# Gated delta rule on one core: five entries of a hand-written slot table moved

## The reference, cut to what matters

```
def step(S, inp):                       # one token; S is 96 x 192 for each of 8 heads
    q_t, k_t, v_t, g_t, b_t = inp
    S = S * jnp.exp(g_t)[..., None, None]
    v_old = jnp.einsum('bhk,bhkv->bhv', k_t, S)
    delta = (v_t - v_old) * b_t[..., None]
    S = S + jnp.einsum('bhk,bhv->bhkv', k_t, delta)
    o_t = jnp.einsum('bhk,bhkv->bhv', q_t, S)
    return (S, o_t)
...
g_out = (h @ Wg).reshape(B, T, H, dv)
o = _rmsnorm(o, onorm_w) * jax.nn.silu(g_out)
x = x + o.reshape(B, T, H * dv) @ Wo
```

## Time and profile before

| | us |
|---|---|
| median of 3 runs | 3595.34 (3591.72 to 3601.11) |
| profiled execution, its own time | 3593.64 |
| its span in the trace | 3591.9 |
| delta stage's stretch with both units and chunks in flight | about 180 to 1400 of the span |

### The profile page before, as it was taken

How to read it: one execution, slowest core, us unless ns; L and a number is a source line. 1 busy time by engine, 2 the same in 40 slices (tenths; PEclk the granted TensorE clock), 3 DMA queues, 4 the chain that set the end, 5 groups by cost and what they waited for, 6 DMA issues and landing times. The chain is left out here.

```text
span 3591.9 us, 86970 instructions
## 1 busy us (share of the span) xinstructions
PE 3217.1 (90%) x32714; PEld 2426.5 (68%) x32714; DVE 2675.9 (74%) x5718; ACT 2061.6 (57%) x4823; POOL 1796.2 (50%) x1631
## 2 busy tenths in 40 slices
PE   4899999999999999798999999987988799899998
PEld 3678888788788888655666566655665466656665
DVE  5677777777777777477777677776999577767775
ACT  3566666666666666325765477623443466536662
POOL 3355555555555555235664366622222566436662
PEclk9699999999999999999999999997999899999999
DMA  4111111111111110142222212231221122222132
GB/s 130 25 27 27 27 26 27 27 29 27 28 28 37 30 26 13 32 121 54 49 70 68 67 46 52 69 97 46 72 63 41 47 53 69 64 72 48 47 75 74
DMA packets 406989, 182.42 MB, mean 51 GB/s; under 512 B 233552, under 2 KB 381744, under 8 KB 404016
## 3 DMA queue, kind: packets, MB, share of 16 engines
q1 hardware_dynamic: 406576, 176.87, 20.1%
HBM read 94.20 MB, written 40.12 MB: 37 GB/s over the span
## 5 line engine op out<-in xcount | busy, mean ns | idle before, releaser
L1205 POOL TENSOR_TENSOR delta_cv<-delta_cv,delta_last_tap 96x256 f32<-96x256 f32 (+1 forms) x384 | 331.8, 864 | 557.0 <-DVE delta_cv L1646 557.0
L1985 POOL TENSOR_TENSOR g_a_rn<-g_a_clip,held_minus_half 128x16 f32<-128x16 f32 x64 | 186.3, 2911 | 240.7 <-DVE g_a_clip L2250 240.7
L1985 POOL TENSOR_TENSOR f_a_rn<-f_a_clip,held_minus_half 128x16 f32<-128x16 f32 x64 | 186.3, 2910 | 237.9 <-DVE f_a_clip L2250 209.7
L2202 ACT ACTIVATE g_a_pr<-g_ps,g_a_nb,g_a_rn 128x128 f32<-128x128 f32 x512 | 185.5, 468 | 125.4 <-DVE g_a_nb L2284 125.4
L2202 ACT ACTIVATE f_a_pr<-f_ps,f_a_nb,f_a_rn 128x128 f32<-128x128 f32 x512 | 185.5, 468 | 124.8 <-DVE f_a_nb L2284 124.8
L1474 ACT ACTIVATE delta_cv<-delta_ps,delta_conv_qk 96x256 f32<-96x256 f32 x256 | 121.4, 474 | 229.6 <-PE delta_ps L1299 228.5
L1638 DVE SCALAR_TENSOR_TENSOR delta_cv<-delta_ps,delta_conv_qk,delta_cv 96x256 f32<-96x256 f32 x256 | 122.1, 477 | 170.8 <-ACT delta_last_tap L1476 168.8
L1243 PE MATMUL delta_ps<-delta_state,delta_qk 96*128 96x192 f32 x1024 | 197.4, 336 | 27.1 <-issue 26.5
L1243 PEld LDWEIGHTS delta_ps<-delta_state,delta_qk 96*128 96x128 f32 x1024 | 164.5, 191 | 37.2 <-issue 33.8
L1988 POOL TENSOR_TENSOR f_a_rot_c<-f_a_rot_c,f_a_rot_s 128x1024 f32<-128x1024 f32 x64 | 150.5, 2351 | 0.0
L1988 POOL TENSOR_TENSOR g_a_rot_c<-g_a_rot_c,g_a_rot_s 128x1024 f32<-128x1024 f32 x64 | 150.4, 2350 | 0.0
(11 more groups left out here) (349 smaller groups left out, 10288.5 us busy)
## 6 DMA issues: line engine op xcount, KB each, us to landing
f_a_vm<-f_a_v SPq DMA_DIRECT2D x128, 130.0 KB, 2.3
g_a_vm<-g_a_v SPq DMA_DIRECT2D x128, 130.0 KB, 2.3
delta_gd<-delta_dram_row SPq DMA_DIRECT2D x16, 1024.0 KB, 4.9
window_vm<-window_v SPq DMA_DIRECT2D x64, 128.0 KB, 2.3
f_m_x<-y SPq DMA_DIRECT2D x24, 256.0 KB, 3.5
delta_dram_inv<-delta_sub SPq DMA_DIRECT2D x16, 256.0 KB, 2.1
f_m_more<-x SPq DMA_DIRECT2D x16, 256.0 KB, 4.1
held_table<-const_rotation SPq DMA_DIRECT2D x4, 1024.0 KB, 6.7
```

The lines of the kernel that those rows point to most:

```text
L1205: pool.tensor_tensor(cv[0:M, t % 3], cv[0:M, t % 3], last_tap[0:M, t % 3], ALU.add).then_inc(summed.sem, 1)
L1985: pool.tensor_tensor(rn[:, u % 2], clip[:, u % 2], minus_half[:], ALU.pow).then_inc(rn_sb.sem, 1)
L2202: e = act.activation(pr[:, u % 2, half, i, :], ps[:, score_bank(u, half), i * P:(i + 1) * P], ACT.Exp, bias=nb[:, u % 2, half, i:i + 1], s ...
```

## The change

Five edits to the table of the delta stage; no instruction is added or removed.

1. The query scores of the second half of the heads (`kq`, i = 1) move from slots 18 and 19 to 21 and 22: on PE eight matmul passes each, on DVE one L1679 each. With them SP's load of the next unit's decays moves from slot 20 to 23.
2. The norms `inv`, `brk`, `nbrk`, `npb` (DVE) move from slot 19 to 20, and `bvr` from 19 to 17.
3. POOL's merge factors `bm` move from slot 22 to 21.
4. For even chunks POOL's power (L1229) moves from slot 21 to 22, and its two norm products (L1236) from 21, 22 to 23, 24.
5. ACT takes the first gate of the odd chunk (slot 22) ahead of `light` instead of behind it.

```
-    KK_AT, KQ_AT = ((6, 7), (9, 10)), ((13, 14), (18, 19))
+    KK_AT, KQ_AT = ((6, 7), (9, 10)), ((13, 14), (21, 22))
+    POWER_AT, NORMED_AT = (16, 15), (17, 15)
...
-                n = unit(t, K_NORM + 8)
+                n = unit(t, K_NORM + 7)
                 if n is not None:
                     rates_sb.need(pool, n)
...
-                C = chunk(t, 15)
-                if C is not None:
-                    ostat_sb.need(pool, C)
-                    o_normed.need(pool, C - 1)
-                    pool.tensor_tensor(of[:], ostat[:, 1, :], minus_half[:, 0:H], ALU.pow).then_inc(of_sb.sem, 1)
...
+                for cc in range(2):
+                    C = chunk_of(t, POWER_AT[cc], cc)
                     if C is not None:
...
+                        pool.tensor_tensor(of[:], ostat[:, 1, :], minus_half[:, 0:H], ALU.pow).then_inc(of_sb.sem, 1)
+                    for i in range(2):
+                        C = chunk_of(t, NORMED_AT[cc] + i, cc)
...
-            def misc(t):
+            def gates(t, ahead):
                 for cc in range(2):
                     for k, when in enumerate(GATE_AT[cc]):
                         C = chunk_of(t, when, cc)
-                        if C is not None:
+                        if C is not None and ahead == (k == 0 and cc == 1):
...
                 products_of(t)
+                gates(t, True)
                 if t > 0:
                     light(t - 1)
+                gates(t, False)
                 misc(t)
...
-                n = unit(t, K_NORM + 5)
+                n = unit(t, K_NORM + 6)
...
+                n = unit(t, K_NORM + 3)
+                if n is not None:
+                    p = n % 2
                     rn_sb.need(dve, n)
                     dve.tensor_tensor(bvr[:, p], rn[:, p], ex[:, BETA, 2 * n:2 * n + 2, :].rearrange("p t h -> p (t h)"),
```

More of the change, by code:

```diff
@@ L1224, in _ @@
                         pool.tensor_tensor(mine, mine, gate[:, HB * i * DV:HB * (i + 1) * DV], ALU.mult).then_inc(o_gated.sem, 1)
-                C = chunk(t, 15)
-                if C is not None:
-                    ostat_sb.need(pool, C)
-                    o_normed.need(pool, C - 1)
-                    pool.tensor_tensor(of[:], ostat[:, 1, :], minus_half[:, 0:H], ALU.pow).then_inc(of_sb.sem, 1)
-                for i in range(2):
-                    C = chunk(t, 15 + i)
-                    if C is not None:
[L1233 to L1237, removed]
+                for cc in range(2):
+                    C = chunk_of(t, POWER_AT[cc], cc)
+                    if C is not None:
+                        ostat_sb.need(pool, C)
+                        o_normed.need(pool, C - 1)
+                        pool.tensor_tensor(of[:], ostat[:, 1, :], minus_half[:, 0:H], ALU.pow).then_inc(of_sb.sem, 1)
+                    for i in range(2):
+                        C = chunk_of(t, NORMED_AT[cc] + i, cc)
+                        if C is not None:
+                            of_sb.need(pool, C)
+                            o_gated.need(pool, C)
+                            mine = o[:, cc, HB * i:HB * i + HB, :]
+                            pool.tensor_tensor(mine, mine, of[:, HB * i:HB * i + HB].unsqueeze(2).to_broadcast([P, HB, DV]), ALU.mult)\
+                                .then_inc(o_normed.sem, 1)
         @block.tensor
@@ L1503, in misc @@
                             emptied(act.activation(gate[:, k * 512:(k + 1) * 512], ps[:, bank, :], ACT.Silu), ("gate", C, k))
+            def misc(t):
                 for cc in range(2):
```

## The result

| | before | after |
|---|---|---|
| median, us (lowest to highest) | 3597.54 (3591.72 to 3601.11), 4 runs | 3686.45 (3676.84 to 3692.95), 4 runs |
| profiled execution: span | 3591.9 | 3690.1 |
| PE busy / idle in the span | 3217.1 / 374.8 | 3276.5 / 413.6 |
| ratio, 95% interval | | 1.0247 (1.0216 to 1.0278) |

A forecast was written before the change was run, and what follows sets the result against it. The prediction took PE, busy 90% of the span, as the bound, with only its idle time to win or lose. Waits +15.0, clock +12.0 and late loads -2.4 gave +24.6 on 3593.6 us: 3618, range 3582 to 3642.

The forecast's parts named there:

- First half of the walk: Around slots 19 and 20, PE idles 0.6 and then 1.75 us instead of 1.33; the second kd wait goes.
- the walk: Unit 7 stepped through in the new order from the old rows: +1.0 us per unit, +15.0 over 15 units.
- The gate waits for DVE: At slot 22's gate, PE waits 2.05 us for DVE to read the scores of slot 21.
- the norms, which now stand in between, add 718.88 - 718.16 = 0.72: On DVE between the taps of slots 20 and 21, the moved norms add 0.72 us.
- The waiting term: PE's waits in units 1 to 15: 15 x 1.0 = +15.0 us, range +9 to +21.
- The clock term: PE's half-clock stretches around the new gaps: 0.8 us per unit, +12.0 in all; bounds 0 and 3.4 per unit.
- Out of that go the two POOL-made waits: After the gate, PE's waits in slots 23 and 24, 1.03 and 1.05 us by start times, disappear.
- Late loads: In units 5 and 14, x4's wait for its DMA and the clock falls behind it go: -2.4 us.
- Rival 1: The walk holds but PE is not throttled by such short gaps: 3607 us, chance 0.20.
- Rivals 2 and 3: Rival 2: no gate wait, 3575 us, chance 0.20; rival 3: waits only change places, 3592 us, chance 0.10.
- rival 2: At slot 22's gate, the scores' bank comes back in time and the kernel is faster: 3575 us, chance 0.20.
- The direction: Whole kernel: slower was given chance 0.57, same 0.23, faster 0.20.

The follow-up runs named there:

- e1: The kernel after with the norms inv, brk, nbrk and npb back in slot 19; 3606.21 us, ratio 1.0026.
- e6: The kernel after with POOL's gate product of 768 columns written as four products of one head each; 3631.24 us, ratio 1.0104.
- e2: The kernel before with the norms edit alone: inv, brk, nbrk, npb in slot 20, bvr in slot 17; 3642.37 us, ratio 1.0118.
- e4: The kernel before with edits 3, 4 and 5 alone, scores and norms in their old slots; 3576.75 us, ratio 0.9940.
- e3: The kernel before with the second scores alone moved to slots 21 and 22; 3610.74 us, ratio 1.0024.
- e5: The kernel after with the second scores back in slots 18 and 19; 3641.12 us, ratio 1.0122.
- e7: e4 with only the odd chunk's second scores moved, from slot 19 to 22; 3608.20 us, ratio 1.0026.
- e12: e4 with only the even chunk's second scores moved, from slot 18 to 22, and the decays' load behind them; 3589.15 us, ratio 0.9978.
- e10: e9 with inv, brk, nbrk and npb in slot 17 instead of 19; 3590.92 us, ratio 0.9979.
- e9: e4 with bm in slot 20, the even chunk's second gate product in slot 21, ACT's first gate waiting for the first product alone; 3579.42 us, ratio 0.9953.

## Why the prediction was right and wrong

- **First half of the walk: right** (0.55 and 1.58 us against 0.6 and 1.75; the second wait for `kd` is gone).
- **"The gate waits for DVE": right in mechanism**, place and releaser. Without the norms between, the walk gives 2.05 - 0.72 = 1.33 us; e1 has 1.06. With a block of 1.35 us (e6) the wait is 1.93, near the 2.05 that the walk has for 0.72.
- **The step that failed: "the norms, which now stand in between, add 718.88 - 718.16 = 0.72".** The duration was taken from slot 19, where POOL did the short instructions of its solve, and carried to slot 20, where POOL does products of 1.80 us. There the block takes 3.3 us on average (4.31 in unit 4), 2.6 more than was put down. The walk moved DVE's instructions along DVE's rows and never laid POOL's beside them, though the order of POOL was at hand. The Trainium skill (SBUF — State Buffer, "SBUF: two separate sides") says that VectorE with two inputs in SBUF and a GpSimd instruction that reads SBUF exclude each other on a shared pair of ports, and whoever starts first keeps it for the whole instruction. The trace agrees: in unit 4 of after `brk` and `npb` end within 0.05 us of POOL's product, in unit 10 a `brk` that starts 0.07 us ahead of it is not held, `npb` is held in full or not at all (e2), and e6 shortens the hold with the instruction.
- **The waiting term, +15.0, measured +38.8** (2.6 us per unit against 1.0). In unit 4 DVE is through with the scores 3.7 us later after the first state products than walked, and PE comes to the gate 1.3 us later than walked, because it went at the half clock on the way: 2.05 + 3.7 - 1.3 is about the 4.40 us of the row. So part of the hold is hidden behind the clock's fall.
- **The clock term, +12, was mis-sized, mostly by the same step.** Measured +59.4, 4.0 per unit, above its upper bound of 3.4. With the norms back (e1) it is +18.3, 1.2 per unit, and with the block at 1.35 us (e6) +24.2, 1.6 per unit: inside the bounds, but half again and twice what was taken. The other 41 that after has above e1 came with the longer gate wait, which brought a half-clock stretch of its own, on the gate and on what follows.
- **"Out of that go the two POOL-made waits": half right.** Both are gone in after, but e4 shows that only the second is of the norm product's making; the first stays there behind POOL's gate product and in after is hidden behind the gate's wait.
- **Waiting, without the hold: the walk's +1.0 per unit less the 0.72 for the norms is +0.3, 4 us in 15 units**; e1 has +2.7.
- **Late loads: right.** `x4` waits for no DMA in the stage of after.
- **Rivals.** Rival 1 (the clock holds) fell: PE is busy 18 to 59 us longer in each kernel that has both scores or the norms of slot 20 in their new slots (after, e1, e2, e3, e5, e6). Rivals 2 and 3 fell with the gate's wait. A gate that does not wait, which rival 2 asked for, is what e7 and e12 have; other waits and the clock take over, and neither gets near its 3575.
- **The direction was partly luck.** "Slower" was forecast without the hold. Without the norms in slot 20 (e1) the kernel is 0.3% slower, on the line of what can be told; with the block at 1.35 us (e6) it is 1% slower. No run has the block in slot 20 at the 0.72 us of the forecast.

## What to carry to other kernels

A duration belongs to its place: before a short DVE instruction with two SBUF inputs is moved, look at what POOL runs there, and count it as long as the rest of POOL's instruction. Split a loss into idle time and busy time first; busy time that grows with the same instruction count points at the clock (PE) or at a held port (DVE). And price edits of a slot table together as well as apart: here three parts of +42, +12 and -23 us made +89.

## What was unexpected in the hardware

- DVE's 128x16 instructions with two SBUF inputs took up to 1.86 us instead of 0.16 to 0.17; a TENSOR_SCALAR with one input (`nbrk`) was held too, 0.65 us under POOL's sum and 1.71 under its product (unit 10 of after) instead of 0.23, while RECIPROCAL (0.24) and TENSOR_REDUCE (0.54) were not. Where both engines' starts lay within 0.02 us, a norm was held in some units and not in others.
- 2.1 us of wait in one piece (e7, e10) cost PE 36.6 and 9.7 us of clock against their neighbours; 1.33 and 0.47 us apart (before, e4, e9) cost next to none, although the sum is about the same. In the 5 us from the first state products on, the granted clock was below 1.00 in 13 of 15 units of e7, in 12 of after, in 8 of e10, and in none of before, e4 and e9; so the length of the wait alone does not decide it. Work that nobody reads bought about 30 us back. The Trainium skill (TensorE: Matmul & The Clock Gate, "HAM oscillation") tells of such falls behind waits for loads; here it fell in most units behind waits of 1.6 to 2.1 us on another engine (after, e7). What exactly decides it was not tried.
